# First attention: the weighted sums of three slots in one group behind the scores of slots 4, 7, 10 and 1

## The reference

```python
x = x + _L0_attn_ref(_layernorm(x), Wq, bq, Wk, bk, Wv, bv, proj)
# 16 heads of 64, causal, 2 sequences of 1024
q = jnp.einsum('bse,hde->bhsd', x, Wq) + bq[None, :, None, :]     # k and v likewise
scores = jnp.einsum('bhsd,bhtd->bhst', q, k) / scale
scores = jnp.where(causal[None, None], -jnp.inf, scores)
att = jax.nn.softmax(scores, axis=-1) / scale
z = jnp.einsum('bhst,bhtd->bhsd', att, v)
return z.reshape(b, s, h * dh) @ proj
```

## Time and profile before

| | us |
|---|---|
| median of 3 runs | 1188.9 |
| lowest and highest of them | 1184.49 and 1189.48 |
| the profiled execution | 1183.85 |
| its span, first to last instruction | 1182.1 |
| mean granted clock of TensorE in it | 0.957 |

### The profile page before, as it was taken

One profiled execution on the slowest core, in us unless ns is written; L12 is line 12 of the kernel. 1 busy time (PEld: TensorE's weight loads), 2 busy tenths in 40 slices (PEclk: granted clock), 3 DMA queues, 4 the chain that ended last, 5 costly groups with the idle time before them and its releaser, 6 DMA issues.

```text
span 1182.1 us, 16993 instructions
## 1 busy us (share of the span) xinstructions
PE 1073.6 (91%) x5839; PEld 585.0 (49%) x5839; DVE 770.8 (65%) x1547; ACT 720.6 (61%) x1173; POOL 541.0 (46%) x446
## 2 busy tenths in 40 slices
PE   3699999999999999999967599999999579999998
PEld 2345555555455555455436322222322257778876
DVE  6767777777777777777635522224221279999998
ACT  3345555655555555555422389998999566656664
POOL 1356666666656666656550000000000026788786
PEclk9789999999999999999886799999999869999999
DMA  4111111111111111111200000000000002122210
GB/s 123 25 25 37 43 26 43 43 27 36 43 26 43 43 34 28 43 35 28 64 1 1 3 8 12 12 10 9 11 12 10 10 0 92 54 72 65 77 53 36
DMA packets 35290, 40.30 MB, mean 34 GB/s; under 512 B 19652, under 2 KB 22484, under 8 KB 34188
## 3 DMA queue, kind: packets, MB, share of 16 engines
q1 hardware_dynamic: 35212, 39.30, 13.0%
HBM read 19.23 MB, written 1.11 MB: 17 GB/s over the span
## 4 chain that ended last, share of the span: by engine, by line
PE 56%; DVE 25%; issue 9%; ACT 5%; SPq 1%; DMA 1%; POOL 1%; DVEq 0%; ACTq 0%; POOLq 0%
PE banks L1007 10%; PE banks L400 8%; PE banks L995 6%; PE banks L385 5%; PE banks L345 5%; DVE qb L1312 5%; PE banks L386 4%; ACT qa L521 3%; PE banks L421 3%; PE banks L366 3%; PE banks L321 3%; DVE qa L583 2%; DVE kb L583 2%; DVE zz L632 2%; PE banks L411 2%
## 5 line engine op out<-in xcount | busy, mean ns | idle before, releaser
L714 POOL TENSOR_TENSOR pacc<-pacc,prob 128x1024 f32<-128x1024 f32 (+3 forms) x160 | 273.9, 1712 | 72.4 <-ACT prob L513 63.1
L1016 ACT ACTIVATE prob<-banks 128x1024 f32<-128x1024 f32 x256 | 238.7, 1099 | 22.4 <-PE banks L995 22.4
L513 ACT ACTIVATE prob<-banks 128x512 f32<-128x512 f32 (+3 forms) x384 | 167.9, 488 | 116.9 <-PE banks L386 114.5
L1345 POOL TENSOR_TENSOR ka<-prob,qb 128x512 fp32r<-128x512 f32 x108 | 165.2, 1550 | 59.5 <-ACT qb L1295 32.9
L385 PE MATMUL banks<-qa,ka 128*128 128x512 f32 (+3 forms) x384 | 155.9, 414 | 5.6 <-ACT prob L513 5.6
L400 PE MATMUL banks<-prob,v 128*64 128x512 f32 (+3 forms) x768 | 146.6, 503 | 1.0 <-POOL prob L705 1.0
L1301 ACT ACTIVATE prob<-banks,w 128x512 f32<-128x512 f32 x144 | 94.5, 686 | 71.4 <-PE banks L1263 71.3
L1007 PE MATMUL banks<-prob,v 128*32 128x512 f32 x1024 | 137.1, 608 | 0.8 <-DVE pacc L1024 0.3
L386 PE MATMUL banks<-qb,kb 72*128 72x512 f32 (+3 forms) x384 | 131.8, 350 | 0.0
L961 POOL TENSOR_TENSOR sq<-sq 64x512 f32<-64x512 f32 x8 | 8.3, 1032 | 259.8 <-DVE sq L957 259.8
L705 POOL TENSOR_SCALAR_AFFINE_SELECT prob<-prob 128x256 f32<-128x256 f32 x128 | 52.0, 406 | 148.3 <-ACT prob L513 146.6
(11 more groups left out here) (211 smaller groups left out, 1629.8 us busy)
## 6 DMA issues: line engine op xcount, KB each, us to landing
qb<-qa SPq DMA_DIRECT2D x64, 128.0 KB, 2.3
ka<-ka SPq DMA_DIRECT2D x64, 128.0 KB, 2.3
prob<-gate_rows SPq DMA_DIRECT2D x8, 1024.0 KB, 4.7
w<-in_experts SPq DMA_DIRECT2D x9, 514.0 KB, 3.5
wqkv<-in_wqkv SPq DMA_DIRECT2D x16, 193.0 KB, 2.4
x<-in_x SPq DMA_DIRECT2D x4, 256.0 KB, 4.3
zz<-pacc SPq DMA_DIRECT2D x64, 16.0 KB
wpr<-pacc SPq DMA_DIRECT2D x64, 16.0 KB
```

Of the source, the lines that this page charges most:

```text
L513: act.activation(pr[:, j % NRING, h, 0:wd], banks[:, h, 0:wd], ACT.Exp, scale=SCALE0).then_inc(s_exp, 1)
L714: pool.tensor_tensor(pacc[:, sbk, :, o:BLK], pacc[:, sbk, :, o:BLK], pr[:, j % NRING, :, 0:wd], ALU.add).then_inc(s_padd, 1)
L1016: act.activation(prob[:, n % NP1, :], banks[:, 2 * (n % 3):2 * (n % 3) + 2, :].rearrange("p b c -> p (b c)"), ACT.Exp, scale=2 * SCALE1).t ...
L1345: pool.tensor_tensor(act2[1][:, tb % 2, i, :], hid[:, tb % 2, i, :], act2[0][:, tb % 2, i, :], ALU.subtract).then_inc(s_hlP, 1)
```

## The change

`unit0_pe` is the only function with another order, and `attn0_pe` follows it at the end of the last unit. The weighted sums now stand in four groups of three slots: 0, 1 and 2 behind the scores of slot 4 (ahead of the raw scores `max_pe` 0 of the next unit), 3, 4 and 5 behind slot 7, 6, 7 and 8 behind slot 10 (ahead of `max_pe` 4), and 9, 10 and 11 behind slot 1 of the next unit. Behind the scores of slots 3, 5, 9 and 11 there are none any more. The instructions are the same ones, and those of ACT, DVE, POOL and SP keep their order.

```diff
@@ attn0_pe
-            for j in (10, 11):
+            for j in (9, 10, 11):
                 pv_pe(pe, u, 1, j, False)
@@ unit0_pe
                 elif j == 1:
                     if not first:
-                        pv_pe(pe, u - 1, x_, 10, first)
-                        pv_pe(pe, u - 1, x_, 11, first)
+                        for i in (9, 10, 11):
+                            pv_pe(pe, u - 1, x_, i, first)
...
-                elif j == 3:
-                    pv_pe(pe, u, w, 0, first)
-                    pv_pe(pe, u, w, 1, first)
-                    if first:
-                        router_const_pe(pe, 0)
+                elif j == 3 and first:
+                    router_const_pe(pe, 0)
                 elif j == 4:
+                    for i in (0, 1, 2):
+                        pv_pe(pe, u, w, i, first)
                     if first:
                         router_const_pe(pe, 1)
                     if not last:
                         max_pe(pe, n, x_, 0)
                 elif j == 5:
-                    pv_pe(pe, u, w, 2, first)
-                    pv_pe(pe, u, w, 3, first)
                     if not first:
                         out_pe(pe, u - 1, False)
...
                 elif j == 7:
-                    pv_pe(pe, u, w, 4, first)
-                    pv_pe(pe, u, w, 5, first)
+                    for i in (3, 4, 5):
+                        pv_pe(pe, u, w, i, first)
...
-                elif j == 9:
-                    pv_pe(pe, u, w, 6, first)
-                    pv_pe(pe, u, w, 7, first)
+                elif j == 9 and not last:
+                    max_pe(pe, n, x_, 3)
+                    turn_pe(pe, n, 0, False)
+                elif j == 10:
+                    for i in (6, 7, 8):
+                        pv_pe(pe, u, w, i, first)
                     if not last:
-                        max_pe(pe, n, x_, 3)
-                        turn_pe(pe, n, 0, False)
-                elif j == 10 and not last:
-                    max_pe(pe, n, x_, 4)
+                        max_pe(pe, n, x_, 4)
                 elif j == 11:
                     if not last:
                         max_pe(pe, n, x_, 5)
-                    pv_pe(pe, u, w, 8, first)
-                    pv_pe(pe, u, w, 9, first)
-                    if not last:
                         v_pe(pe, n, x_, bn, 0)
                         max_pe(pe, n, x_, 6)
```

## The result

The changed kernel takes 1218.54 us in the median of four runs (1215.17 to 1219.47), the kernel before 1188.1 beside it: a ratio of **1.0268, 95% interval 1.0246 to 1.0289** (the two medians alone give 1.0256), some 30 us slower. The profiled execution took 1219.47 us with a span of 1217.6, 35.5 us more than the one before.

The account below looks back on a forecast made before the run. PE, busy 34.17 of a unit's 35.23 us, sets the pace; new waits and moved work less savings give 1.17 us a unit, 15 x 1.17 = +17.5 us, 1201.4 or 1206.4 by base, 1205 taken; range 1194 to 1230.

Parts of the forecast that it names:

- the sum: All units of the first attention: 15 x 1.17 us, +17.5 us in all; its own range 1193 to 1212 us.
- Price of a group: Weighted sums on PE: opening a group costs about 0.16 us; two fewer save 0.37 us a unit with the way in.
- Slots 2 to 5: PE stands empty 1.36 us ahead of scores 4 until mrow ends; the wait ahead of out goes, out +0.05 us.
- Slots 9 to 11 and 1: PE empty 0.88 us ahead of scores 10 for slot 9's exponential; +0.57 us at unit end, +0.64 in next slot 1.
- The unit: One unit of the first attention gets longer: +1.21 us by one count, +1.12 by another, 1.17 taken.
- Rival (A), the clock: New PE waits bring the granted clock to 0.50, 3.4 us each; 27 us on top if half the units fall; chance 0.08.
- (B): Slot 10 doesn't wait, its cover being longer than reckoned; 1.08 us goes, +0.1 us a unit, 1190 us; chance 0.08.
- (C): ACT and DVE pieces run shorter without PV beside them; at 40% shorter -0.7 us a unit, 1178 us; chance 0.05.
- What was costed at nothing: Ring of six prob buffers: exponentials of slots 9 and 3 need PV 3 and PV 9; 0.2 us a unit if cover failed.

Follow-up runs that it names:

- the five groups: Kernel before with PV 8 and 9 moved from behind scores 11 to behind scores 1 of the next unit: 1183.70 us, ratio 0.9968.
- the half alone: Kernel before with only PV 0 to 5 regrouped (under Slots 2 to 5), 1196.62 us, or only PV 6 to 11 (under Slots 9 to 11 and 1), 1209.69 us.
- both waits filled: Changed kernel with idle matmuls behind scores 3 and behind max 3 of slot 9, inside both new waits: 1202.52 us, ratio 1.0131.
- The fillers: Changed kernel with idle matmuls in the wait ahead of scores 4 (1214.45 us), ahead of scores 10 (1210.49 us), or in both (1202.52 us).
- the first wait filled: Changed kernel with two idle matmuls behind scores 3, inside the wait ahead of scores 4: 1214.45 us, ratio 1.0238.
- mrow first: Changed kernel with mrow taken by DVE ahead of the subtraction of the next unit's first projection: 1210.59 us, ratio 1.0200.
- the early half: Kernel before with PV 0 to 2 behind scores 4 and PV 3 to 5 behind scores 7, the rest unmoved: 1196.62 us, ratio 1.0101.
- the late half alone: Kernel before with PV 6 to 8 behind scores 10 and PV 9 to 11 behind scores 1 of the next unit: 1209.69 us, ratio 1.0198.
- the second filled: Changed kernel with one idle matmul of 320 columns behind max 3 of slot 9, ahead of scores 10: 1210.49 us, ratio 1.0210.

## Why the prediction was right, and where it was too low

It said slower, 1205 us, range 1194 to 1230. Measured were 1218.54. Sign and range hold; the loss was 30 us where the sum had 17.5. The range of the sum itself, 1193 to 1212, doesn't hold the result. It is in the range only because that was stretched to 1230 for a rival with a chance of 0.08, and this rival came true together with the forecast. Point by point:

- *Price of a group:* 0.16 us for opening and 0.05 on the way, 0.37 for two. By the five groups it is 0.12 each, 0.24 for two. A little too high. The rule of the Trainium skill (TensorEngine Tiling (Array Packing), Key Properties) that a change of tiling mode drains TensorE goes the right way: a group less saves these 0.12 us. That the drain is what they pay for, no run here shows. By that rule alone the change would have been a gain, and it was a loss.
- *Slots 2 to 5:* a wait of 1.36 forecast, 1.35 from start to start, with mrow at its end; out +0.05 forecast, +0.07 found; the half alone +0.26 against +0.29.
- *Slots 9 to 11 and 1:* 0.88 us forecast ahead of scores 10, 0.91 found; from scores 9 to PV 6 the forecast has 3.24 us, found are 3.23 (336.80 to 340.03); PV 6 to 8 2.74 against 2.72; the half alone +0.94 against +0.96.
- *The unit:* +1.17 against +1.23 to 1.25, at full clock. With both waits filled so that the clock stays up, the kernel takes 16.8 us more; the forecast had 17.5. So the sum was right for a kernel whose clock stays up.
- *Rival (A), the clock:* this is the step that failed. I gave it 0.08, on the ground that one wait of 1.31 us elsewhere left the clock at 1.00. One such row showed that a fall need not come, not that it doesn't. The changed kernel has the wait 14 times, and 11 falls come behind it. I also looked at the longer wait alone and not at the 0.9 us of slot 10, which is followed by falls too. The price of a fall was too high, 3.4 us from the row of the last unit, against 1.66: the low clock lasts 6.7 us there and 3.4 here. For half of the units (A) had 27 us; the 13 falls that came cost 21. And (A) came on top of the forecast, it was no alternative to it.
- *Rivals (B) and (C):* the wait of slot 10 is there, 0.67 us on the record. DVE's pieces took 1.51 us for the pair of line 577 and 1.28 for that of mrow, as before. Mrow had PV beside it then and finds PE empty now, so (C) is out. (One reason that the forecast gave against (C) was misread: PV lies beside the subtraction at 338.04 only up to 338.4, not for half of it.)

```profile
354.11 1.51 DVE L577 SCALAR_TENSOR_TENSOR qa<-banks,wqkv,qa 64x512 fp32r<-64x512 f32 x2 [0.97 <-ACT qa L515]
355.65 1.28 DVE L606 TENSOR_TENSOR qb<-banks,mD 8x512 fp32r<-8x512 f32 x2
```

- *What was costed at nothing:* no record shows PE or ACT in wait for PV 3 or PV 9. The waits of the changed kernel do put 35.6 us of ACT's idle time, 16 times, down to POOL's sums (line 708), which the kernel before doesn't have. That is the exponential of slot 6, and POOL isn't what holds it: it needs the sums of slot 0 only, which are long over, and starts at 365.17, 0.13 us behind the matmuls of its own scores.

What stays open: why a wait of the same length is followed by a fall in one unit and not in the next, and why 0.67 us in slot 10 are enough while 0.90 us ahead of scores 4 are not. The fillers show that the idle time is a cause. For the second question two answers are left, and no run parts them: the kind of work around the wait (narrow scores, raw scores and a transpose in slots 9 and 10, wide scores in slot 4), or the idle time nearby taken together, 0.3 + 0.67 us against 0.90. For the first, the regular order of the falls with the first wait filled and with mrow first suggests that the moment of the wait counts beside its length. None of this is shown.

## What to carry to other kernels

Work that is gathered into fewer, larger groups leaves its cover where it was: ask of each place that loses a group what the next instruction waits for, follow that chain back to an anchor that doesn't move, and compare with what a group less is worth, here 0.12 us against waits of 1.35 and 0.9 us. The wait ahead of out that went in exchange has to be counted too; here it left +0.29 us for the early half and +0.96 for the late one. Where a PE that was never idle gets a repeated wait of about a microsecond, price the lower clock behind it as well, by the number of places. And where a chain through another engine sets a start, its order on that engine may be the cheaper thing to change: mrow ahead of one subtraction gave 10.5 us, 7.7 of them in the units, where one group less gave 0.12 us a unit.

## What the runs showed of the hardware that I had not expected

- In the late half alone PE waits twice close together in every unit, 0.3 us ahead of scores 9 and 0.67 ahead of scores 10, and is busy otherwise but for the 0.74 us ahead of out. The granted clock fell from 1.00 to 0.50 behind these waits in seven of 14 units, and each fall cost about 1.65 us. With both new waits filled it fell in none.
- The falls move between two places of waiting: with both waits 11 come behind the first and 2 behind the second; with the first filled 9 behind the second, with the second filled 7 behind the first, with both filled none.
- Idle matmuls inside two waits made a kernel faster: 16.8 us over the kernel before in place of 30.4, ratios of 1.0131 and 1.0268.
